# Choosing key chunks by comparison and a running count instead of match-and-replace, with a tanh output gate and casts on ScalarE

## The reference

```
q, k = rope(x Wq), rope(x Wk);  v = x Wv          # 32 heads of 8
kmean = mean of k over each chunk of 32 tokens     # 16 chunks
gate  = q . kmean;  future chunks -> -1e30, own chunk -> +1e30
allowed = the 4 chunks with the largest gate (the own one among them), causal inside
o = softmax(q k / sqrt(8) where allowed) v
o = o * rsqrt(mean(o^2) + 1e-6) * o_norm_weight * sigmoid(x Wg1 Wg2)
x1 = layernorm(x + o Wo)
out = layernorm(x1 + x1 + shared experts(x1) + sum over 4 of 16 experts of gate_e * relu(x1 W1_e + b) W2_e)
```

## Time and profile before

| | |
|---|---|
| median of three runs | 1691.63 us (1689.74 to 1695.02) |
| the profiled execution | 1689.1 us |
| its span, first to last instruction | 1687.3 us |
| PE busy | 88% of the span |
| DVE busy | 81% |
| ACT, POOL busy | 47%, 32% |
| mean granted TensorE clock | 0.931 of full speed |
| one turn with experts | about 198 us |

### The profile page before, as it was taken

One profiled execution on the slowest core, in us unless ns is written; L12 is line 12 of the kernel. 1 busy time (PEld: TensorE's weight loads), 2 busy tenths in 40 slices (PEclk: granted clock), 3 DMA queues, 4 the chain that ended last, 5 costly groups with the idle time before them and its releaser, 6 DMA issues.

```text
span 1687.3 us, 31401 instructions
## 1 busy us (share of the span) xinstructions
PE 1481.0 (88%) x11488; PEld 792.2 (47%) x11488; DVE 1374.0 (81%) x4523; ACT 796.8 (47%) x1010; POOL 540.0 (32%) x638
## 2 busy tenths in 40 slices
PE   5688899898998989988999989989899898998597
PEld 3332455435554455534655355543555345552254
DVE  6995888878898788987989788987889879898534
ACT  4319352573527543383534835266442845339221
POOL 3104422253223532244222532234422343225132
PEclk8758899998999989998999989999899998999799
DMA  6000000000000000000000000000000000000000
GB/s 218 1 0 2 26 2 1 1 26 14 1 1 14 14 14 1 1 14 26 1 1 1 26 14 1 1 14 14 14 1 2 13 14 1 1 1 14 13 1 13
DMA packets 15633, 22.73 MB, mean 13 GB/s; under 512 B 940, under 2 KB 12886, under 8 KB 15224
## 3 DMA queue, kind: packets, MB, share of 16 engines
q1 hardware_dynamic: 15480, 20.74, 3.8%
HBM read 16.54 MB, written 4.19 MB: 12 GB/s over the span
## 4 chain that ended last, share of the span: by engine, by line
PE 50%; DVE 33%; DVEq 5%; ACT 5%; issue 4%; POOL 2%; DMA 1%; SPq 0%; POOLq 0%; ACTq 0%
PE PS L482 12%; PE PS L465 11%; DVE rep L1102 7%; PE PS L398 6%; PE PS L619 5%; DVE CM L1095 3%; DVEq L984 2%; PE PS L473 2%; ACT UQ L846 2%; PE PS L389 2%; PE PS L629 2%; DVE CM L1161 2%; DVE hr L991 2%; PE PS L415 2%; DVE qT L1187 2%
## 5 line engine op out<-in xcount | busy, mean ns | idle before, releaser
L896 POOL TENSOR_TENSOR hp<-hr,hp 128x512 f16<-128x512 f32 (+1 forms) x200 | 230.8, 1154 | 709.2 <-ACT hp L735 485.6
L1161 DVE TENSOR_REDUCE CM<-PS 128x32 f32<-128x1024 f32 x320 | 385.1, 1222 | 45.7 <-PE PS L398 40.5
L482 PE MATMUL PS<-W,hp 128*128 128x256 f16 (+1 forms) x2400 | 314.2, 276 | 18.0 <-POOL hp L896 18.0
L465 PE MATMUL PS<-x1T,W 128*128 128x512 f16 (+1 forms) x1200 | 316.2, 393 | 0.8 <-ACT hr L726 0.8
L726 ACT ACTIVATE hr<-PS,CF 128x512 f32<-128x512 f32 (+1 forms) x200 | 137.3, 687 | 346.1 <-PE PS L473 316.9
L482 PEld LDWEIGHTS PS<-W,hp 128*128 128x128 f16 (+1 forms) x2400 | 215.9, 98 | 92.2 <-issue 44.3
L991 DVE TENSOR_TENSOR hr<-hr,PS 128x512 f32<-128x512 f32 x176 | 120.3, 684 | 74.0 <-ACT hr L726 67.3
L846 ACT ACTIVATE UK<-PS 128x1024 f32<-128x1024 f32 x160 | 153.8, 1034 | 22.1 <-PE PS L415 20.1
L465 PEld LDWEIGHTS PS<-x1T,W 128*128 128x128 f16 (+1 forms) x1200 | 110.5, 101 | 113.9 <-issue 32.5
L846 ACT ACTIVATE UQ<-PS 128x1024 f32<-128x1024 f32 x160 | 152.2, 1044 | 4.4 <-PE PS L415 2.5
L735 ACT ACTIVATE hp<-hr 128x512 f16<-128x512 f32 (+1 forms) x122 | 77.1, 632 | 160.4 <-DVE hr L991 158.9
(11 more groups left out here) (138 smaller groups left out, 2189.1 us busy)
## 6 DMA issues: line engine op xcount, KB each, us to landing
xT<-in_xT SPq DMA_DIRECT2D x8, 512.0 KB, 3.8
v<-in_x SPq DMA_DIRECT2D x8, 512.0 KB, 3.8
out<-x1n SPq DMA_DIRECT2D x8, 512.0 KB, 2.9
qET<-in_w SPq DMA_DIRECT2D x1, 1664.0 KB, 21.2
UK<-in_w SPq DMA_DIRECT2D x1, 1584.0 KB, 8.1
UQ<-in_w SPq DMA_DIRECT2D x1, 1584.0 KB, 11.4
kz<-in_w SPq DMA_DIRECT2D x1, 1536.0 KB, 19.9
WA<-in_wa SPq DMA_DIRECT2D x1, 776.0 KB, 5.3
```

What stands on the lines that cost most here:

```text
L465: mm = pe.matmul(PS[0:w, BK_H, :], W1[:, a, k, bass.ds(f0, w)], x1T[:, e, k, :], start=(n == 0), stop=(n == 5))
L482: mm = pe.matmul(PS[:, BK_Y + j // 2, (j % 2) * D:(j % 2 + 1) * D], hp[0:w, slot, a, j * P:(j + 1) * P], W2[0:w, e, bass.ds(c, 1), :].rear ...
L896: nc.gpsimd.tensor_tensor(hp[0:w, slot, 1, :], hr[0:w, slot, :], hp[0:w, slot, 0, :], ALU.subtract).then_inc(pool_hp, 1)
L1161: nc.vector.tensor_reduce(dst, src, AX.X, ALU.max).then_inc(dve_cm, 1)
```

## The change

Four things change.

1. `mark` is gone. `select(j)` now takes the third largest gate of every head as a threshold, marks equal gates (`eq`) and smaller ones (`under`), works out how many of the equal ones are needed, and finds the first so many of them by a running count over the 512 columns, restarted at each head (`tensor_tensor_scan` with the factor 0 at a head's first column). From these it makes `cbias`. Two tables are added to the constants CH, which grow from 192 to 768 f16 columns.
2. `best` is cut into two halves of 16 heads, and the order of DVE becomes: half, `gate_next`, half, `gate_next`, `select`, `gate_next`, for each tile. So chunk 3 is multiplied inside tile 1 and no longer after it.
3. In the selection stretch the cast of the gated chunk moves from DVE to ACT, behind the two evictions of the step.
4. ACT evicts the output gate by `tanh(x / 2)`; `sigmoid` is gone, and its addition and factor go into two instructions that are there already.

```diff
+                        if m is not None:
+                            high(m, c, (C_TOPK[0] + u) % 2)
...
-                    nc.scalar.activation(eg[:, 2 * i:2 * i + 2, :].rearrange("p t d -> p (t d)"), PS[:, i, :], ACT.Exp,
-                                         scale=-1.0).then_inc(act_eg, 1)
+                    nc.scalar.activation(eg[:, 2 * i:2 * i + 2, :].rearrange("p t d -> p (t d)"), PS[:, i, :], ACT.Tanh,
+                                         scale=0.5).then_inc(act_eg, 1)
...
-            def best(b, j, bank):
...
-            def mark():
-                link(nc.vector.memset(top8[:, :, TOPK - 1:8], PAD))
-                for h in range(H):
-                    nc.vector.match_replace(rep[:, h, :], top8[:, h, :], gmask[:, h, :], CHOSEN)
-            def select(j):
-                dve.drain()
-                link(nc.vector.scalar_tensor_tensor(out=cbias[:, j], in0=rep[:, :, 0:NCH], scalar=BIG,
-                                                    in1=sm_c[:, j:j + 1, :].to_broadcast([P, H, NCH]),
-                                                    op0=ALU.is_le, op1=ALU.mult))
+            def best(b, j, bank, part):
+                if part == 0:
+                    dve.wait_ge(pe_gate, b * 3 + j + 1)
+                    nc.vector.tensor_tensor(gmask[:, :, :], PS[:, bank, :].rearrange("p (h n) -> p h n", n=NCH),
+                                            gm_c[:, j:j + 1, :].to_broadcast([P, H, NCH]), ALU.add).then_inc(dve_gm, 1)
+                    dve.drain()
+                for h in range(part * H // 2, (part + 1) * H // 2):
+                    nc.vector.max(top8[:, h, :], gmask[:, h, :])
+            def select(j):
                 dve.drain()
+                thr, need, same = want[:, 0, :], want[:, 1, :], want[:, 2, :]
+                eq, under, count = flag[:, 0], flag[:, 1], flag[:, 2]
+                wide = lambda t: t.unsqueeze(2).to_broadcast([P, H, NCH])
+                nc.vector.tensor_scalar(thr, top8[:, :, TOPK - 2], -BIG / 2, None, ALU.max)
+                nc.vector.tensor_tensor(same, top8[:, :, 0], top8[:, :, 2], ALU.is_equal)
+                link(nc.vector.tensor_tensor(need, top8[:, :, 1], top8[:, :, 2], ALU.is_equal))
+                nc.vector.tensor_tensor(eq, gmask[:, :, :], wide(thr), ALU.is_equal)
+                nc.vector.scalar_tensor_tensor(out=need, in0=need, scalar=1.0, in1=same, op0=ALU.add, op1=ALU.add)
+                link(nc.vector.tensor_tensor(under, gmask[:, :, :], wide(thr), ALU.is_lt))
+                link(nc.vector.tensor_tensor(eq[:, :, 0], eq[:, :, 0], need, ALU.subtract))
+                link(nc.vector.tensor_tensor_scan(count.rearrange("p h n -> p (h n)"), inner,
+                                                  eq.rearrange("p h n -> p (h n)"), 0.0, ALU.mult, ALU.add))
+                link(nc.vector.scalar_tensor_tensor(out=eq, in0=count, scalar=0.0, in1=eq, op0=ALU.is_gt, op1=ALU.mult))
+                link(nc.vector.tensor_tensor(under, under, eq, ALU.add))
+                link(nc.vector.tensor_tensor(cbias[:, j], under, sm_h[:, j:j + 1, :].to_broadcast([P, H, NCH]), ALU.mult))
...
-                        gated(m, c, c % 2, split=True)
+                        gated(m, c, c % 2)
...
-                best(b, 1, 3)
-                mark()
-                select(1)
-                gate_next()
-                for j, bank in ((2, 0), (3, 1)):
-                    best(b, j, bank)
+                for j, bank in ((1, 3), (2, 0), (3, 1)):
+                    best(b, j, bank, 0)
                     gate_next()
-                    mark()
+                    best(b, j, bank, 1)
                     gate_next()
                     select(j)
-                    gate_next()
-                for _ in range(*C_TOPK):
                     gate_next()
...
-                sigmoid(0)
...
-                    link(nc.vector.tensor_tensor(sq, u8, tok(ry).unsqueeze(3).to_broadcast([P, NT, 2 * HG, HD]), ALU.mult))
+                    link(nc.vector.scalar_tensor_tensor(out=sq, in0=u8, scalar=0.5 * HD ** 0.5,
+                                                        in1=tok(ry).unsqueeze(3).to_broadcast([P, NT, 2 * HG, HD]),
+                                                        op0=ALU.mult, op1=ALU.mult))
                     eg_4 = eg_i.rearrange("p t (h d) -> p t h d", d=HD)
-                    link(nc.vector.scalar_tensor_tensor(out=eg_4, in0=sq, scalar=HD ** 0.5, in1=eg_4,
-                                                        op0=ALU.mult, op1=ALU.mult).then_inc(dve_on, 1))
+                    link(nc.vector.scalar_tensor_tensor(out=eg_4, in0=eg_4, scalar=1.0, in1=sq,
+                                                        op0=ALU.add, op1=ALU.mult).then_inc(dve_on, 1))
...
-                sigmoid(1)
+                dve.wait_ge(act_eg, b * 2 + 2)
```

More of the change, by code:

```diff
@@ L80 @@
 C_W = C_B1 + NC
-H_ID, H_IND, H_W = 0, 128, 192
+H_ID, H_IND, H_RST, H_SM, H_W = 0, 128, 192, 704, 768
 G_ID, G_CQ, G_W = 0, 128, 384
@@ L123, in build @@
         eg = qT[:, :, :].rearrange("p k s -> p (k s)").rearrange("p (t d) -> p t d", t=NT)
-        gmask = sb("gmask", [P, H, TOPW])
+        gmask = sb("gmask", [P, H, NCH])
+        flag = sb("flag", [P, 3, H, NCH], F16)
+        want = sb("want", [P, 3, H])
         rep = sb("rep", [P, H, TOPW])
@@ L179, in build @@
         ind = CH[:, H_IND:H_IND + 64].rearrange("p (t n) -> p t n", t=NT)
+        inner = CH[:, H_RST:H_RST + H * NCH]
+        sm_h = CH[:, H_SM:H_SM + 64].rearrange("p (t n) -> p t n", t=NT)
         identb = CG[:, G_ID:G_ID + P]
@@ L964, in _ @@
             dve.wait_ge(s_const, 16 * N_CONST)
-            nc.vector.memset(gmask[:, :, NCH:TOPW], PAD)
             nc.vector.memset(PS[:, BK_PV, :], 0.0)
@@ L1086, in block_diagonal @@
                         bmask.unsqueeze(2).to_broadcast([P, 16, NCH]), ALU.mult).then_inc(dve_kb, 1)
-            def best(b, j, bank):
-                dve.wait_ge(pe_gate, b * 3 + j + 1)
-                nc.vector.tensor_tensor(gmask[:, :, 0:NCH], PS[:, bank, :].rearrange("p (h n) -> p h n", n=NCH),
-                                        gm_c[:, j:j + 1, :].to_broadcast([P, H, NCH]), ALU.add).then_inc(dve_gm, 1)
-                dve.drain()
-                for h in range(H):
-                    nc.vector.max(top8[:, h, :], gmask[:, h, 0:NCH])
-                dve.drain()
@@ L1181, in turn @@
                         gated(m, C_BIAS[0] + j - 2, (C_BIAS[0] + j - 2) % 2)
-                def sigmoid(i):
-                    settled_wait(dve, act_eg, b * 2 + i + 1)
-                    e2 = eg[:, 2 * i:2 * i + 2, :].rearrange("p t d -> p (t d)")
-                    link(nc.vector.tensor_scalar(e2, e2, 1.0, None, ALU.add))
-                    link(nc.vector.reciprocal(e2, e2))
-                sigmoid(0)
                 if m is not None:
@@ L1290 @@
     ch[:, H_IND:H_IND + 64] = np.where(n == own, UNIT, 0.0).reshape(P, -1)
+    ch[:, H_RST:H_RST + H * NCH] = np.arange(H * NCH) % NCH != 0
+    ch[:, H_SM:H_SM + 64] = np.where(n == own, 0.0, -OFF).reshape(P, -1)
     cg = np.zeros((P, G_W), f32)
```

## The result

| | before | after |
|---|---|---|
| median | 1690.68 us (4 runs, 1684.15 to 1695.02) | 1720.45 us (4 runs, 1720.15 to 1722.09) |
| ratio, 95% interval | | 1.0181 (1.0147 to 1.0216) |
| span of the profiled execution | 1687.3 us | 1718.4 us |
| DVE busy | 81% | 73% |
| mean granted TensorE clock | 0.931 | 0.921 |

The change costs 1.8%, though DVE has less to do.

What follows compares the result with a forecast made beforehand. PE bounds the maxima stretch, so delay from DVE's selections is kept: 4.5 + 1.2 - 0.2 = 5.5 us in turns 1 to 7, +1 in turn 0, together +40. Profiled 1729, median 1731, range 1698 to 1752.

Steps and rivals of the forecast that it cites:

- PE is the bound behind the selection, and what enters late stays late: Maxima stretch: PE is busy 61.00 of 61 us at full clock, so any delay with which it enters is kept.
- The first `gated` is asked for too early: Tile 1: DVE reaches `gated(3)` at 612.1, PE not before 618.21, so DVE stands idle for 7.3 us.
- the walk's d3, d4, d5 and d10: Selection stretch, turn 3: forecast starts of `gated` for chunks 3, 4, 5 and 10, at 619.42, 623.35, 630.55 and 650.87.
- S = 6.6: Price of one new selection on DVE, from the `gated` before it to the one after: 5.5 us plus 1.1 for POOL.
- the rival of two passes: Scan of the selection takes two passes, 0.53 us more: selection 7.1, shift 6.1, +51, 1743 us; chance 22%.
- The collision with POOL, once per tile: Selection: one DVE instruction reading two SBUF tensors waits about 1.1 us for POOL's `low` in each of three tiles.
- The shift of 4.5 us: End of the selection stretch: PE's third maxima unit waits for DVE's first reduction and starts 4.5 us later per turn.
- The clock, 1.2 us a turn (0 to 1.6): Maxima stretch: after PE stands about 4.4 us, half speed during some 2.4 us costs 1.2 us.
- The gate, 0.2 us a turn: Output gate: without the second reciprocal `copy_outputs(1)` can come 0.2 us earlier, saving 0.2 per turn.
- the second reciprocal was on the path in full: Rival at the output gate: 3.1 us less per turn than forecast, 1709 us; chance 6%.
- Turn 0, +1: Turn 0, without chunks: three selections save about 0.5 us each, the first meets POOL's work, constants are larger: +1.
- No load of function tables: ACT: exp and tanh share one table set, so no load; rival of two loads a turn, +18, 1749 us, 4%.

Runs made afterwards that it cites:

- e3: The changed kernel, but DVE does all of tile 1 (mask, maxima, selection) before it asks for the first gated chunk: 1676.53 us, 0.9926 of the kernel before.
- e5: The changed kernel with PE repeating the `up` matmuls of chunk 11 three times while it would wait for DVE: 1714.12 us, 1.0142 of the kernel before.
- e8: The changed kernel without the scan (no running count, the product reads the marks themselves): 1689.13 us, 0.9990 of the kernel before.
- e1: The kernel before with the tanh gate alone, no sigmoid on DVE: 1683.55 us, ratio 0.9959.
- e11: The kernel before without the second of the two reciprocals of the output gate: 1685.25 us, ratio 0.9983.
- e9: The changed kernel with the scan done twice, same output: 1769.07 us, 1.0468 of the kernel before.
- e12: The kernel before without the first of the two reciprocals of the output gate: 1693.27 us, ratio 1.0018.
- e4: The changed kernel with the old match-and-replace in place of the count, new order, casts and tanh gate kept: 1711.80 us, 1.0124 of the kernel before.
- e6: The changed kernel with tile 1 whole first and the count of tiles 2 and 3 cut ahead of the scan, between chunks: 1669.18 us, 0.9880 of before.
- e7: The changed kernel with tile 1 whole first and match-and-replace for the count, cut after 16 heads in tiles 2 and 3: 1649.44 us, 0.9764 of before.

## Why the prediction was right

The forecast was 1731 (1698 to 1752), slower with 0.84; measured 1720.45. Step by step:

- **PE is the bound behind the selection, and what enters late stays late.** Right. The maxima stretch is 58.33 us in every kernel whose PE enters busy, and in no kernel less.
- **The first `gated` is asked for too early.** Right: DVE idle for 7.74 us (forecast 7.3, turn 3), and e3, which mends this alone, gets 44 us back. Counted from the first `gate_of`, the walk's d3, d4, d5 and d10 were 1.21, 5.14, 12.34 and 32.66; the trace has 1.21, 5.14, 12.22 and 32.42.
- **S = 6.6.** Measured 6.48, by luck: errors cancel. The scan takes 1.225 us and not 0.69: the rival of two passes, and 0.69 + 0.53 = 1.22 was its price, +0.53. The sum and the last product, with f16 on all sides (L1121, L1122), take 0.426, the lower bound; that gives 0.27 back at the sum, but only 0.03 at the product, since `gated` starts 0.58 after it. The subtraction with its collision is 0.20 shorter than forecast, the drain and the small instructions 0.13. The rule of the Trainium skill that the scan runs at half throughput (DVE: opcode table, instruction layouts, handler registers and perf-mode slots, Datapath and trigger behaviour) is right here; taken alone, without the fast f16, it would have put S at 7.1.
- **The collision with POOL, once per tile.** Right in kind and number, though the sign given for it, an instruction of 1.7 us or more, didn't come, as a short one was hit: L1117 takes 1.10 in the median, and 0.29 where nothing meets it, so 0.8 for a forecast of 1.1; POOL's `low` is longer too where they meet, 1.39 for 1.15. The source view of L1117: least, median and most ns.
```profile
L1117 DVE TENSOR_TENSOR flag<-flag,want x24: 294/1092/1102, 50.1 to 1476.0; 128x32 f16<-128x32 f16 x24
```
- **The shift of 4.5 us.** Measured 4.13 in turn 3, and 3.84 in the mean, since turns of before differ (36.63 to 38.05). `gate_of` waits 1.12 and 1.12 (forecast 1.3), `down` 0.51 behind each.
- **The clock, 1.2 us a turn (0 to 1.6).** Mis-sized: 1.79 in the mean, above its own bound. Half speed was put at 2.4 us of PE's work; in turn 3 PE worked at it for 3.86 us (window 669:673). The mechanism is shown by e5, and turn 7 of e8 shows that it doesn't always set in.
- **The gate, 0.2 us a turn.** The term that was mis-sized most. The probabilities stretch gives 1.12 us a turn, and e1 alone 1.35. The step that failed reads "it can come 0.2 earlier": true of that copy (0.34 in turn 3, 0.08 in the mean), but the norm chain behind it and the next copy, where 1.14 lie, weren't followed. The rival that the second reciprocal was on the path in full is wrong all the same: 3.1 more was never there, and e11 gives 0.62 of 3.35.
- **Turn 0, +1.** Measured +0.3, for the same reason: its third unit comes 1.9 later (72.70 for 70.81), and its probabilities stretch gives 1.9 back (51.75 for 53.65).
- **No load of function tables.** Right; ACT's groups still show one (before: the earlier trace rows).
```profile
L711 ACT ACT_TABLE_LOAD x1 | 1.3, 1283 | 8.0 <-DMA CG<-in_cg 8.0
```

Forecast and measurement by term, seven turns: shift 31.5 and 26.9; clock 8.4 and 12.5; gate -1.4 and -8.6 (with the stretch behind it); turn 0 1 and 0.3; together 39.5 and 31.1. Of the 8.4 us too much the gate has 7.2, the shift 4.6 and turn 0 0.7, less 4.1 of clock. The rest up to 1731 is rounding and the 2.5 us between profiled execution and median, which the changed kernel doesn't have (1720.40 and 1720.45). So the total is nearer than its terms: the direction rests on the walk, which came out, and the size in part on a clock too small and a gate too small, of opposite sign.

## What to carry to other kernels

Ask not what work costs on its engine but what stands behind its last part: here DVE was less busy by 8% of the span in the slower kernel, and the place of two calls was worth 44 us. Do what needs nothing from the bound engine before that engine arrives, put the waits for it between equal portions of the rest, and prefer few instructions with two SBUF inputs where POOL works beside them. Follow a saved microsecond to the second consumer, and keep PE's wait apart from its shift against the old kernel: here the low clock came behind the wait, not with the shift.

## What the hardware showed beyond that

- A wait of PE can cost more than it lasts. Behind idle times of 4.17 us (after) and 2.87 us (e8) at the third unit the clock was 1.2 GHz for some 3 to 4 us, for 1.8 and 1.25 us a turn; behind the waits of 1.12 us in the selection stretch `down` kept its 1.48 us. The same 2.87 us did nothing in turn 7 of e8, and in turn 3 of e9 a wait of 2.57 us brought the low clock and one of 2.40 didn't. Useless matmuls in the wait removed the loss (e5).
- Instructions of 32 columns on DVE, 0.18 to 0.21 us by themselves, took 0.46 to 0.67 beside causal masks on POOL; 0.34 us of phase decided how many met them. One input was no protection: L1001 (DVE, e12) starts 0.10 after three masks of POOL begin, and takes 0.58 instead of 0.18.
```profile
747.32 0.58 DVE L1001 TENSOR_SCALAR rep<-rep 128x32 int32<-128x32 int32 x1
```
  The copies out of PSUM stayed at 0.69. The Trainium skill (SBUF — State Buffer, Who interferes with whom) names both kinds, two SBUF inputs and the two-port mode of `tensor_scalar`. The traces agree with the first (L1216 above, 0.67); the second fits L1001, but no row shows in which mode an instruction ran.
- MAX8 and match-and-replace were not slowed beside `low` (means of 160 to 172 ns a head beside it, 160 to 176 away from it, in before, after, e4, e6 and e7), while `low` cost the count 0.8 us in each tile.
- A sum (L1121), or a product with one input broadcast (L1122), took 0.43 us for 512 columns with f16 on all sides; `scalar_tensor_tensor` with f16 on all sides took 0.69 (L1120), as L1111 of e7 did with an f32 input.
